# Two expert phases of a fused attention and expert network: choosing spread over units, low parts on GpSimd, a count copied by ScalarE, a weight load moved ahead, variances moved

## The chip, the cores and the metric

One core of one Trainium2 chip runs the whole program. The time is the device time of one execution in microseconds. Three executions of the kernel before took 2613.11, 2613.51 and 2613.93 us.

## The reference, cut to what matters

Two layers act on a residual x of 2048 rows (4 batches of 512) by 256.

```python
x = x + attention(layernorm(x), ctx)          # 16 heads of 64, 1024 context rows of 192, softmax
h = layernorm(x)                              # layer 0: 32 experts of width 128, 2 shared chunks
s = sigmoid(h @ gate.T); c = s + bias         # groups of 4: the best 4 of 8 groups, then the best 6 experts
w = chosen(s, c); w = 2.5 * w / sum(w)
x = x + sum_e w[:, e] * (silu(h @ g_e) * (h @ u_e)) @ d_e + shared(h)
x = x + attention(layernorm(x), ctx)
h = layernorm(x)                              # layer 1: 8 experts of width 512, 4 shared chunks
e = argmax(h @ router.T)                      # one expert a row
x = x + (silu(h @ g_e) * (h @ u_e)) @ d_e + shared(h)
```

## The kernel before, in words

The program runs five phases one behind the other, each a block with a barrier at its end: attention of layer 0 (tag L0a), experts of layer 0 (L0e), attention of layer 1 (L1a), shared experts and routing of layer 1 (L1e), and the routed experts of layer 1 on rows sorted by expert (L1s). Every fp32 operand of a product is split into a high part (a ScalarE copy to fp32r, a "_hi" tile) and a low part (a subtraction, "_lo"), and each product is three matmuls.

**Expert phase** (expert_phase). The weights come in chunks of 128 hidden columns, two buffers (raw[0] and raw[1]); four blocks of 512 rows each make a unit, so unit u is chunk u // 4 and block u % 4. Units are written out up to unit 9 and then looped eight at a time, or written out to unit 15 in layer 1. For a unit TensorE does gate_up (12 matmuls, L1365) into PSUM bank u % 2 and 2 + u % 2, ScalarE the silu of the gate (act_g, L1113), VectorE the product hid (L1176, counted by the semaphore mul), ScalarE the high part hid_hi (L1116, hhi), VectorE the low part hid_lo (L1181, hlo), and TensorE down (12 matmuls, L1379) of the unit two before; VectorE adds the result, weighted, to the residual (add, L1168, fma). gate_up(u) waits for mul of unit u - 2; down(u) waits for hlo of unit u and for the add of unit u - 2. VectorE's order in a unit is mul, add(u - 2), hid_lo. The weights of a chunk are split by ScalarE (split, L1102) at units 2, 6, 10, ... ahead of the silu, and by GpSimd (w_lo, L1083 and L1087); SyncE's queue loads the next chunk when w_lo has been made. In layer 1 the same queue carries two loads of 6 MB (prefetch) for the sorted phase.

**Choosing.** choose() is a Python generator of VectorE instructions that pick the experts, each linked to the one before it by a semaphore wait (link). In layer 0 it ends with the weights of the experts, which the adds need from unit 8 on. In layer 1 it goes on into sort_tokens: TensorE counts the rows of each expert (count, three matmuls into bank 1, L1393 and L1395), VectorE copies the counts out (L1231, L1232, semaphore taken), TensorE waits for that copy before gate_up(5), and more VectorE work makes slot_of, by which GpSimd scatters the rows to HBM at the end of its list (L1093). STEPS says how many pieces of the generator run ahead of which unit: those pieces stand before the unit's mul.

**Start of the phase.** ScalarE loads the square root's table (L1132), then makes rt_hi, the high part of the router (L1135); VectorE does four bn_stats (L1308), then rt_lo (L1310), for which TensorE's first matmuls (route, L1404) wait. raw[1] is loaded behind the bias, the sorted_x wipe of layer 0, and in layer 1 behind the first 6 MB.

**Attention phase** (attention_phase). A segment is a batch and a pair of heads, 32 in a phase, some 26 us each. VectorE's order in segment i is: low keys, statistics, variance at step 2 of a batch (ROOT, L578 to L583), inner_scales at step 3 (L590 to L592), outer_scales at step 4 (L596 to L598), then normalise, high and low output of segment i - 1 (L535 to L548), queries (L504, L509), low_rows, add_output (L558) and four row maxima (L530). GpSimd adds up the probabilities of the softmax in 14 additions of 128x512 (L326) in the middle of a segment.

Of the kernel before, what the change touches and what calls it, by code (L numbers as in the profile page):

```python
# [46 lines left out]
def build(nc, x, ctx_top, ctx_bot, layer_in, out):  # L47
# [6 lines left out]
    with stack:  # L54
# [37 lines left out]
        def attention_phase(tag, weights, value_weights, bias, xres, prefetch, source=None, again=False, keep=False, clear=()):  # L92

            with scope() as s:
# [29 lines left out]
                with nc.Block() as block:  # L124
# [373 lines left out]
                    def _(dve):  # L498
# [128 lines left out]
                        def segment(i):  # L627
# [9 lines left out]
                            if step == ROOT:  # L637
                                variance(b)
                            if step == INNER:
                                inner_scales(b)  # L640
                            if step == OUTER:
                                outer_scales(b)
# [9 lines left out]
                            if i + 1 < SEGMENTS:  # L652
                                high_queries(i + 1)
                                low_queries(i + 1)
                            if i > 0:
# [296 lines left out]
        def expert_phase(tag, cfg, bias, packed, xres, dispatch=None, prefetch=(None, None), wipe=None, clear=()):  # L952
# [9 lines left out]
            with scope() as s:  # L962
# [46 lines left out]
                with nc.Block() as block:  # L1009
# [20 lines left out]

                    def rest(eng, unit):

                        done = cfg["shared"] * BLK
                        first = -(-(done - 2) // ROUND)
                        for u in range(done, min(first * ROUND + 2, UNITS)):
                            unit((u - 2) // ROUND, (u - 2) % ROUND + 2)
# [4 lines left out]
                        if done < UNITS:  # L1041
# [4 lines left out]
                    def _(sp):  # L1046
                        if G:
# [9 lines left out]
                        sp.dma_start(raw[1], packed[1, :, :]).then_inc(sem["raw1"], 16)  # L1057
# [11 lines left out]
                    def _(pool):  # L1069
# [14 lines left out]
                        with pool.Fori(1, chunks // 2) as j:  # L1084
                            for par in range(2):
                                pool.wait_ge(sem["whi"], j * 2 + (par + 1))
                                nc.gpsimd.tensor_tensor(w_lo[:, par, :], raw[par], w_hi[:, par, :], ALU.subtract)\  # L1087
                                    .then_inc(sem["wlo"], 1)
# [10 lines left out]
                    def _(act):  # L1099
# [4 lines left out]
                        def unit(j, u):  # L1104
                            k = j * ROUND
                            if u % BLK == 2 and not (isinstance(j, int) and j == ROUNDS - 1 and u == ROUND - 2):
# [25 lines left out]
                        nc.scalar.activation(junk[:, :], ones[:, 0:1], ACT.Sqrt)  # L1132
                        act.wait_ge(sem["rt"], 16)
                        act.wait_ge(sem["pad"], 2)
                        nc.scalar.activation(rt_hi[:, :, 0:E], rt, ACT.Copy).then_inc(sem["rhi"], 1)  # L1135
                        split(0, 0)
# [10 lines left out]
                        unit(0, 0)  # L1147
                        unit(0, 1)
# [8 lines left out]
                    def _(dve):  # L1157
# [40 lines left out]
                        def pick(v, k, n, eq, gt, sel, start):  # L1198
# [6 lines left out]
                            if G:  # L1205
                                yield
# [557 lines left out]
```

## Time and profile before

| | us |
|---|---|
| median of three runs | 2613.51 |
| the profiled execution | 2618.82 |
| its span, first to last instruction | 2616.9 |
| TensorE busy | 2520.7 (96%) |
| VectorE busy | 2091.2 (80%) |
| GpSimd busy | 1482.1 (57%) |
| ScalarE busy | 1246.1 (48%) |

Times of the trace are microseconds from the span's start. The mean granted clock of TensorE is 0.985 of full speed over the span. A busy share of 96% says that TensorE almost never stands still; what it does wait for is found in the view of waits and in its timeline, where a bracket behind an instruction gives the idle time ahead of it and what ended that.

### The profile page before, as it was taken

Reading aid. Unit: us, or ns where it says so; the run is one execution under the profiler, and the core shown is the slowest. Engines: PE = TensorE matmul, PEld = TensorE weight load, DVE = VectorE, ACT = ScalarE, POOL = GpSimd, SP = SyncE. Lnnn points to the kernel's source line nnn. Section 1 sums busy time; section 2 is a strip of 40 time slices with the busy share of each in tenths; the row PEclk is TensorE's granted clock in tenths of the full one; section 3 lists DMA queues with packets and bytes.
Section 4 is the critical chain, followed back from the end, with each engine's and each line's share of the span. In section 5 each row is a group of like instructions: output and inputs, shape, how many; then the busy total and the mean of one; then the engine's idle time right before and its main releaser. Section 6 shows DMA issues by size and latency. Waiting matters only on the chain. (4 is left out here: it accounts for less than half of the span.)

```text
span 2616.9 us, 37958 instructions
## 1 busy us (share of the span) xinstructions
PE 2520.7 (96%) x13304; PEld 1776.5 (68%) x13304; DVE 2091.2 (80%) x2602; ACT 1246.1 (48%) x1774; POOL 1482.1 (57%) x1124
## 2 busy tenths in 40 slices
PE   8999999999999889999999899999999999998795
PEld 6666565656665678888888766666666665656684
DVE  7888888888888487777777788888888888866695
ACT  5555555555554323333333355455555454533393
POOL 5878777877777311111111187687878777760345
PEclk9999999999999999999999999999999999999897
DMA  4122212222221200000000121222131222115112
GB/s 147 45 59 53 63 45 58 63 49 50 63 51 41 72 19 24 24 24 24 24 24 18 47 75 45 55 61 59 45 79 45 59 53 55 45 29 235 47 54 88
DMA packets 118648, 145.09 MB, mean 55 GB/s; under 512 B 63856, under 2 KB 80112, under 8 KB 117488
## 3 DMA queue, kind: packets, MB, share of 16 engines
q1 hardware_dynamic: 113664, 136.10, 19.3%
q0 software_dynamic: 1536, 4.20, 0.5%
q10 hardware_dynamic: 3312, 3.02, 0.3%
q8 instruction: 81, 1.33, 0.2%
q14 instruction: 55, 0.45, 0.1%
HBM read 80.93 MB, written 11.80 MB: 35 GB/s over the span
## 5 line engine op out<-in xcount | busy, mean ns | idle before, releaser
L326 POOL TENSOR_TENSOR L1a_psums<-L1a_psums,L1a_probs 128x512 f32<-128x512 f32 x384 | 479.1, 1293 | 0.0
L326 POOL TENSOR_TENSOR L0a_psums<-L0a_psums,L0a_probs 128x512 f32<-128x512 f32 x384 | 478.8, 1289 | 0.0
L530 DVE TENSOR_REDUCE L1a_row_max<-psum 128x2 f32<-128x2048 f32 x128 | 293.6, 2293 | 59.2 <-PE psum L796 58.9
L530 DVE TENSOR_REDUCE L0a_row_max<-psum 128x2 f32<-128x2048 f32 x128 | 293.5, 2293 | 57.7 <-PE psum L796 57.2
L400 ACT ACTIVATE L0a_probs<-psum 128x1024 f32<-128x1024 f32 x256 | 251.6, 1027 | 105.9 <-PE psum L819 105.7
L400 ACT ACTIVATE L1a_probs<-psum 128x1024 f32<-128x1024 f32 x256 | 251.6, 1027 | 105.1 <-PE psum L819 104.9
L1168 DVE SCALAR_TENSOR_TENSOR xres<-psum,L0e_weights_of,xres 128x256 f32<-128x256 f32 x544 | 225.6, 478 | 22.6 <-PE psum L1379 21.7
L833 PE MATMUL psum<-L1a_probs,L1a_v 128*64 128x512 f32 x1024 | 240.5, 601 | 0.0
L833 PE MATMUL psum<-L0a_probs,L0a_v 128*64 128x512 f32 x1024 | 240.4, 601 | 0.0
L1365 PE MATMUL psum<-xnT_hi,L0e_w_hi 128*128 128x512 f32 x544 | 215.0, 395 | 9.4 <-DVE L0e_hid L1176 9.4
L1365 PE MATMUL psum<-xnT_lo,L0e_w_hi 128*128 128x512 f32 x544 | 214.6, 394 | 0.0
L1365 PE MATMUL psum<-xnT_hi,L0e_w_lo 128*128 128x512 f32 x544 | 213.1, 392 | 0.0
L818 PE MATMUL psum<-L0a_q_hh,L0a_k_st 128*128 128x512 f32 x512 | 204.4, 399 | 1.4 <-ACT L0a_probs L400 0.9
L818 PE MATMUL psum<-L1a_q_hh,L1a_k_st 128*128 128x512 f32 x512 | 204.3, 399 | 1.4 <-ACT L1a_probs L400 0.9
L819 PE MATMUL psum<-L1a_q_lm,L1a_k_hs 65*128 65x512 f32 x512 | 203.1, 397 | 0.0
L819 PE MATMUL psum<-L0a_q_lm,L0a_k_hs 65*128 65x512 f32 x512 | 203.0, 397 | 0.0
L1113 ACT ACTIVATE L0e_act_g<-psum 128x512 f32<-128x512 f32 x136 | 81.3, 598 | 243.4 <-PE psum L1365 243.4
L558 DVE TENSOR_TENSOR xres<-psum,xres 128x512 f32<-128x512 f32 x128 | 88.6, 692 | 114.9 <-PE psum L708 113.8
L1176 DVE TENSOR_TENSOR L0e_hid<-psum,L0e_act_g 128x512 f32<-128x512 f32 x136 | 93.7, 689 | 102.8 <-ACT L0e_act_g L1113 102.7
L326 POOL TENSOR_TENSOR L1a_psums<-L1a_probs 128x512 f32<-128x512 f32 x64 | 82.4, 1307 | 153.5 <-ACT L1a_probs L400 153.5
L1087 POOL TENSOR_TENSOR L0e_w_lo<-L0e_raw,L0e_w_hi 128x768 fp32r<-128x768 f32 x16 | 30.0, 1875 | 242.1 <-ACT L0e_w_hi L1102 242.1
L1087 POOL TENSOR_TENSOR L0e_w_lo<-ctx_stage,L0e_w_hi 128x768 fp32r<-128x768 f32 x16 | 30.6, 1914 | 240.9 <-ACT L0e_w_hi L1102 240.9
(384 smaller groups left out, 6148.6 us busy)
## 6 DMA issues: line engine op xcount, KB each, us to landing
L0a_k_hs<-L0a_k_st SPq DMA_DIRECT2D x64, 256.0 KB, 3.6
L1a_k_hs<-L1a_k_st SPq DMA_DIRECT2D x64, 256.0 KB, 3.7
L0a_raw<-in_attention SPq DMA_DIRECT2D x33, 384.0 KB, 3.4
L1a_raw<-in_attention SPq DMA_DIRECT2D x33, 384.0 KB, 3.4
L1weights<-in_sorted SPq DMA_DIRECT2D x2, 6144.0 KB, 20.6
L0a_q_hh<-L0a_q_hh SPq DMA_DIRECT2D x64, 128.0 KB, 2.3
L1a_q_hh<-L1a_q_hh SPq DMA_DIRECT2D x64, 128.0 KB, 2.3
ctx_stage<-in_experts SPq DMA_DIRECT2D x19, 384.0 KB, 3.0
```

The lines of the kernel that those rows point to most:

```text
L326: nc.gpsimd.tensor_tensor(psums[:, h, :], a, probs[:, h, kv, :], ALU.add).then_inc(sem["acc"], 1)
L400: nc.scalar.activation(probs[:, h, 2 * kp:2 * kp + 2, :], slot(h).rearrange("p (n q) -> p n q", n=2), ACT.Exp, scale=SCALE)\
L530: nc.vector.reduce_max(row_max[:, qt, 0:33:32], psum[:, 0:4 * BANK].rearrange("p (h k) -> p h k", h=2), axis=AX.X).then_inc(sem["max"], 1)
L558: nc.vector.tensor_tensor(rows, bank(PLACE[f"OUT{half}"]), rows, ALU.add).then_inc(sem["added"], 1)
L818: nc.tensor.matmul(dst, k_st[:, par, h, keys_of], q_hh[:, par, h, :], start=True, stop=False)
L819: last = nc.tensor.matmul(dst, k_hs[0:DH + 1, par, h, keys_of], q_lm[0:DH + 1, par, h, :], start=False, stop=True)
L833: last = nc.tensor.matmul(O[HEAD[h], :], v[:, pair % 2, kv, cols], probs[:, h, kv, :], start=kv == 0, stop=kv == KVT - 1)
L1087: nc.gpsimd.tensor_tensor(w_lo[:, par, :], raw[par], w_hi[:, par, :], ALU.subtract)\
L1113: nc.scalar.activation(act_g[:, u % 2, :], bank(u % 2), ACT.Silu).then_inc(sem["silu"], 1)
L1168: last = nc.vector.scalar_tensor_tensor(acc, bank(4 + 2 * (u % 2) + n // 2)[:, (n % 2) * DIM:(n % 2 + 1) * DIM], weights_of[:, ds(j * (2 * ...
L1176: nc.vector.tensor_tensor(hid[:, u % 2, :], bank(2 + u % 2), act_g[:, u % 2, :], ALU.mult)\
L1365: last = nc.tensor.matmul(bank(2 * g + u % 2), a[:, par, w], m[:, kd, rows], start=n == 0, stop=n == 3 * KD - 1)
```

## The change

1. The choosing of a phase is cut into eight pieces (layer 0) or seven (layer 1), one in each unit from unit 2 on, and a piece runs behind the unit's mul and ahead of its add, where it ran ahead of the mul before.
2. In units 2 to 9 (HELPED) GpSimd makes hid_lo; VectorE's mul of unit u then waits for hlo of unit u - 2. The w_lo of chunk 2 comes in GpSimd's list ahead of unit 6's hid_lo, that of chunk 3 behind unit 9's.
3. In layer 1 count goes into bank 0, behind gate_up(5), once the mul of unit 4 has been done; ScalarE makes both copies behind its unit 4; TensorE waits for them before gate_up(6), with down(3) in between.
4. raw[1] is the first DMA of the expert phase in SyncE's queue, and its split stands behind ScalarE's unit 0 instead of at unit 2.
5. rt_hi comes ahead of the square root's table load, and rt_lo ahead of the bn_stats.
6. In attention variance, inner_scales and outer_scales run behind the queries' low parts instead of ahead of normalise.

```diff
--- before.py
+++ after.py
@@ -634,12 +634,6 @@
                 statistics(b, step)
-            if step == ROOT:
-                variance(b)
-            if step == INNER:
-                inner_scales(b)
-            if step == OUTER:
-                outer_scales(b)
             if i == 0:
@@ -652,6 +646,12 @@
                 low_queries(i + 1)
+            if step == ROOT:
+                variance(b)
+            if step == INNER:
+                inner_scales(b)
+            if step == OUTER:
+                outer_scales(b)
             if i > 0:
@@ -1028,22 +1028,29 @@
+    SHARED_UNITS = cfg["shared"] * BLK
+    SINGLE = min(-(-(SHARED_UNITS - 2) // ROUND) * ROUND + 2, UNITS)
+    HELPED = range(2, 10)
+    COUNTED = 5
     def rest(eng, unit):
-        done = cfg["shared"] * BLK
-        first = -(-(done - 2) // ROUND)
-        for u in range(done, min(first * ROUND + 2, UNITS)):
-            unit((u - 2) // ROUND, (u - 2) % ROUND + 2)
+        first = -(-(SHARED_UNITS - 2) // ROUND)
         if first < ROUNDS - 1:
                     unit(j, u)
-        if done < UNITS:
+        if SHARED_UNITS < UNITS:
             for u in range(2, ROUND):
     def _(sp):
+        sp.dma_start(raw[1], packed[1, :, :]).then_inc(sem["raw1"], 16)
         if G:
@@ -1054,7 +1061,6 @@
                          zeros[:, :].unsqueeze(1).broadcast_to([P, wipe.shape[0] // P, DIM])).then_inc(sem["wiped"], 16)
-        sp.dma_start(raw[1], packed[1, :, :]).then_inc(sem["raw1"], 16)
         with sp.Fori(1, chunks // 2) as j:
@@ -1081,11 +1087,23 @@
         nc.gpsimd.tensor_tensor(w_lo[:, 1, :], raw[1], w_hi[:, 1, :], ALU.subtract).then_inc(sem["wlo"], 1)
-        with pool.Fori(1, chunks // 2) as j:
-            for par in range(2):
-                pool.wait_ge(sem["whi"], j * 2 + (par + 1))
-                nc.gpsimd.tensor_tensor(w_lo[:, par, :], raw[par], w_hi[:, par, :], ALU.subtract)\
-                    .then_inc(sem["wlo"], 1)
+        def low_weights(j, par):
+            pool.wait_ge(sem["whi"], j * 2 + (par + 1))
+            nc.gpsimd.tensor_tensor(w_lo[:, par, :], raw[par], w_hi[:, par, :], ALU.subtract)\
+                .then_inc(sem["wlo"], 1)
+        for u in HELPED:
+            if u % BLK == 2 and u > BLK and u < SHARED_UNITS:
+                low_weights(*divmod(u // BLK + 1, 2))
+            pool.wait_ge(sem["hhi"], u + 1)
+            nc.gpsimd.tensor_tensor(hid_lo[:, u % 4, :], hid[:, u % 2, :], hid_hi[:, u % 4, :], ALU.subtract)\
+                .then_inc(sem["hlo"], 1)
+        low_weights(1, 1)
+        if chunks > 4:
+            with pool.Fori(2, chunks // 2) as j:
+                for par in range(2):
+                    low_weights(j, par)
         if dispatch is not None:
@@ -1103,7 +1121,7 @@
             k = j * ROUND
-            if u % BLK == 2 and not (isinstance(j, int) and j == ROUNDS - 1 and u == ROUND - 2):
+            if u % BLK == 2 and not (isinstance(j, int) and (j, u) in ((0, 2), (ROUNDS - 1, ROUND - 2))):
                 c = u // BLK + 1
@@ -1129,10 +1147,10 @@
-        nc.scalar.activation(junk[:, :], ones[:, 0:1], ACT.Sqrt)
         act.wait_ge(sem["rt"], 16)
         nc.scalar.activation(rt_hi[:, :, 0:E], rt, ACT.Copy).then_inc(sem["rhi"], 1)
+        nc.scalar.activation(junk[:, :], ones[:, 0:1], ACT.Sqrt)
         split(0, 0)
@@ -1145,12 +1163,21 @@
         unit(0, 0)
+        split(0, 1)
         unit(0, 1)
                              ACT.Sigmoid if G else ACT.Copy).then_inc(sem["scores"], 1)
-        first_round(act, unit)
+        if dispatch is not None:
+            for u in range(2, COUNTED):
+                unit(0, u)
+            act.wait_ge(sem["counted"], 1)
+            nc.scalar.activation(held[:, :, :], bank(0)[:, NT * E:2 * NT * E].rearrange("p (t e) -> p e t", e=E), ACT.Copy)\
+                .then_inc(sem["taken"], 1)
+            nc.scalar.activation(gt[:, :, :], bank(0, NT * E).rearrange("p (t e) -> p t e", e=E), ACT.Copy)\
+                .then_inc(sem["taken"], 1)
+        first_round(act, unit, COUNTED if dispatch is not None else 2)
         other_rounds(act, unit)
@@ -1172,11 +1199,20 @@
             k = j * ROUND
+            number = k + u if isinstance(j, int) else None
             dve.wait_ge(sem["silu"], k + (u + 1))
+            if number is not None and number - 2 in HELPED:
+                dve.wait_ge(sem["hlo"], number - 1)
             nc.vector.tensor_tensor(hid[:, u % 2, :], bank(2 + u % 2), act_g[:, u % 2, :], ALU.mult)\
                 .then_inc(sem["mul"], 1)
+            if number in STEPS:
+                next(choosing, None)
             if u >= 2:
                 add(j, u - 2)
+            if number in HELPED:
+                return
+            if number == HELPED.stop:
+                dve.wait_ge(sem["hlo"], HELPED.stop)
             dve.wait_ge(sem["hhi"], k + (u + 1))
@@ -1202,15 +1238,13 @@
             link(last)
-            if G:
-                yield
+            yield
             kth = top[:, :, k - 1:k].broadcast_to([P, NT, n])
             link(nc.vector.tensor_scalar(need[:, :], need[:, :], -1.0, float(k), ALU.mult, ALU.add))
-            if G:
-                yield
+            yield
@@ -1221,19 +1255,14 @@
             nc.vector.memset(start[:, :, 0:1], 0.0).then_inc(sem["picked"], 1)
+            yield
             link(nc.vector.memset(index[:, :], 1.0))
             yield
-            dve.wait_ge(sem["counted"], 1)
-            link(nc.vector.tensor_copy(held[:, :, :], bank(1)[:, NT * E:2 * NT * E].rearrange("p (t e) -> p e t", e=E)))
-            nc.vector.tensor_copy(gt[:, :, :], bank(1, NT * E).rearrange("p (t e) -> p t e", e=E))\
-                .then_inc(sem["taken"], 1)
-            dve.wait_ge(sem["taken"], 1)
-            yield
+            dve.wait_ge(sem["taken"], 2)
             link(nc.vector.tensor_tensor_scan(upto[:, :, :].rearrange("p e t -> p (e t)"),
@@ -1304,10 +1333,10 @@
+        dve.wait_ge(sem["rhi"], 1)
+        nc.vector.tensor_tensor(rt_lo[:, :, 0:E], rt, rt_hi[:, :, 0:E], ALU.subtract).then_inc(sem["rlo"], 1)
         for n in range(NT - TAIL):
             nc.vector.bn_stats(stats[:, n, :], xres[:, TAIL + n, :]).then_inc(sem["stat"], 1)
-        dve.wait_ge(sem["rhi"], 1)
-        nc.vector.tensor_tensor(rt_lo[:, :, 0:E], rt, rt_hi[:, :, 0:E], ALU.subtract).then_inc(sem["rlo"], 1)
         dve.wait_ge(sem["stat"], NT - TAIL)
@@ -1336,13 +1365,12 @@
         choosing = choose()
-        STEPS = {3: 1, 4: 1, 5: 2, 6: 2, 7: 2} if G else {3: 1, 5: 1, 6: 2, 7: 1}
-        for u in range(cfg["shared"] * BLK):
-            for _ in range(STEPS.get(u, 0)):
-                next(choosing, None)
+        STEPS = range(2, 10) if G else range(2, 9)
+        for u in range(SINGLE):
             unit(u // ROUND, u % ROUND) if u < 2 else unit((u - 2) // ROUND, (u - 2) % ROUND + 2)
             pass
+        dve.wait_ge(sem["hlo"], HELPED.stop)
         rest(dve, unit)
@@ -1387,14 +1415,13 @@
             pe.wait_ge(sem["const"], 2)
-            pe.wait_ge(sem["mul"], 2 + 4)
+            pe.wait_ge(sem["mul"], 2 + COUNTED)
             pe.wait_ge(sem["picked"], 1)
             picked = sel[:, :, :].rearrange("p t e -> p (t e)")
-            nc.tensor.matmul(bank(1)[:, 0:NT * E], earlier, picked, start=True, stop=True)
+            nc.tensor.matmul(bank(0)[:, 0:NT * E], earlier, picked, start=True, stop=True)
             for part in (slice(0, DH), slice(DH, P)):
-                last = nc.tensor.matmul(bank(1)[part, NT * E:2 * NT * E], ones[:, :], picked, start=True, stop=True)
+                last = nc.tensor.matmul(bank(0)[part, NT * E:2 * NT * E], ones[:, :], picked, start=True, stop=True)
             last.then_inc(sem["counted"], 1)
-            pe.wait_ge(sem["taken"], 1)
@@ -1444,8 +1471,11 @@
         if dispatch is not None:
+            gate_up(0, COUNTED)
             count()
-        first_round(pe, unit, 5)
+            down(0, COUNTED - 2)
+            pe.wait_ge(sem["taken"], 2)
+        first_round(pe, unit, COUNTED + (dispatch is not None))
         other_rounds(pe, unit)
```

## Rows read from the trace of the kernel before

**Rows 1.** The page's busy times of the whole span.

```profile
PE 2520.7 (96%) x13304; PEld 1776.5 (68%) x13304; DVE 2091.2 (80%) x2602; ACT 1246.1 (48%) x1774; POOL 1482.1 (57%) x1124
```

**Rows 2.** TensorE's waits, whole span: total us, times, longest us.

```profile
PE psum L1365 <- DVE L0e_hid L1176: 9.4, 5, 4.1
PE psum L1379 <- DVE L1e_hid_lo L1181: 4.7, 1, 4.7
...
PE psum L708 <- DVE L0a_o_split L548: 3.2, 5, 1.1
...
PE psum L708 <- DVE L1a_o_split L548: 1.6, 3, 0.6
```

**Rows 3.** Timeline of TensorE, L0e: gate_up of units 4, 8, 10 and 12.

```profile
911.20 0.47 PE L1365 MATMUL psum<-xnT_hi,L0e_w_hi 128*128 128x512 f32 x1 [1.08 <-DVE L0e_hid L1176]
...
938.46 0.47 PE L1365 MATMUL psum<-xnT_hi,L0e_w_hi 128*128 128x512 f32 x1 [4.15 <-DVE L0e_hid L1176]
...
948.95 0.40 PE L1365 MATMUL psum<-xnT_hi,L0e_w_hi 128*128 128x512 f32 x1
...
957.31 0.40 PE L1365 MATMUL psum<-xnT_hi,L0e_w_hi 128*128 128x512 f32 x1
```

**Rows 4.** VectorE in L0e: muls of units 2, 6, 7, 8; a scan.

```profile
910.37 0.69 DVE L1176 TENSOR_TENSOR L0e_hid<-psum,L0e_act_g 128x512 f32<-128x512 f32 x1 [7.53 <-ACT L0e_act_g L1113]
...
934.18 1.23 DVE L1215 TENSOR_TENSOR_SCAN L0e_sel<-L0e_start,L0e_eq 128x512 f32<-128x512 f32 x1
...
937.62 0.69 DVE L1176 TENSOR_TENSOR L0e_hid<-psum,L0e_act_g 128x512 f32<-128x512 f32 x1
...
943.92 0.69 DVE L1176 TENSOR_TENSOR L0e_hid<-psum,L0e_act_g 128x512 f32<-128x512 f32 x1
...
946.69 0.69 DVE L1176 TENSOR_TENSOR L0e_hid<-psum,L0e_act_g 128x512 f32<-128x512 f32 x1
```

**Rows 5.** The first instructions of L0e on ScalarE and GpSimd: rt_hi, the pads.

```profile
885.90 0.24 ACT L1135 ACTIVATE L0e_hid_lo<-ctx_stage 128x64 fp32r<-128x64 f32 x1
...
884.57 0.57 POOL L1072 MEMSET L0e_hid_lo<- 128x256 f32 x2 [10.11 <-POOLq L124]
```

**Rows 6.** Timeline of ScalarE, L0e: split of chunk 1 and the silu's table.

```profile
907.59 0.84 ACT L1102 ACTIVATE L0e_w_hi<-L0e_raw 128x768 fp32r<-128x768 f32 x1
908.44 1.28 ACT L1113 ACT_TABLE_LOAD   x1
```

**Rows 7.** VectorE and GpSimd at the same time in L0e.

```profile
931.02 2.20 DVE L1209 TENSOR_TENSOR L0e_eq<-L0e_choice,L0e_late 128x512 f32<-128x512 f32 x1
...
929.69 2.98 POOL L1087 TENSOR_TENSOR L0e_w_lo<-ctx_stage,L0e_w_hi 128x768 fp32r<-128x768 f32 x1 [19.34 <-ACT L0e_w_hi L1102]
```

**Rows 8.** Timeline of L1e: split; gate_up 4, count, gate_up 5 and 6.

```profile
2382.61 0.84 ACT L1102 ACTIVATE L1e_w_hi<-L1e_raw 128x768 fp32r<-128x768 f32 x1 [2.45 <-DMA L1e_raw<-in_experts]
...
2385.41 0.50 PE L1365 MATMUL psum<-xnT_hi,L1e_w_hi 128*128 128x512 f32 x1 [2.49 <-POOL L1e_w_lo L1083]
...
2392.82 0.46 PE L1393 MATMUL psum<-L1e_sel,ctx_stage 128*128 128x128 f32 x2 [1.36 <-issue]
...
2398.23 0.80 PE L1365 MATMUL psum<-xnT_hi,L1e_w_hi 128*128 128x512 f32 x1 [4.58 <-DVE L1e_gt L1232]
...
2404.79 0.39 PE L1365 MATMUL psum<-xnT_hi,L1e_w_hi 128*128 128x512 f32 x1
```

**Rows 9.** Timeline, L0a: VectorE in a ROOT and the next segment, then GpSimd.

```profile
298.69 1.49 DVE L578 TENSOR_TENSOR L0a_total_of<-L0a_stats 128x8 f32<-128x8 f32 x1
...
300.98 3.36 DVE L535 RECIPROCAL L0a_inv<-psum 128x512 f32<-128x512 f32 x1
...
310.67 1.40 DVE L558 TENSOR_TENSOR xres<-psum,xres 128x512 f32<-128x512 f32 x2 [1.42 <-PE psum L708]
...
336.89 1.40 DVE L558 TENSOR_TENSOR xres<-psum,xres 128x512 f32<-128x512 f32 x2 [2.25 <-PE psum L708]
...
303.82 14.97 POOL L326 TENSOR_TENSOR L0a_psums<-L0a_psums,L0a_probs 128x512 f32<-128x512 f32 x12
```

## The prediction

> **What bounds the kernel now.** The page's busy times come first: TensorE works 96% of the span [rows 1]. An edit that only unloads another engine is worth nothing but where TensorE waits for it. So the view of TensorE's waits comes next [rows 2]: 9.4 us for VectorE's products in L0e, 4.7 us at the end of L1e, and waits of 0.53 us each for o_split, four in L0a ((3.2 - 1.1) / 4; the 1.1 is the phase's last segment) and three in L1a. The timeline of TensorE shows what those waits cost with what follows them. In L0e, gate_up(10) starts at 948.95 and gate_up(12) at 957.31, so an undisturbed unit takes 4.18 us; the six from gate_up(4) at 911.20 should take 25.1 us and took 37.75 [rows 3]: 12.7 us are lost. In L1e, gate_up(4) starts at 2385.41 and gate_up(6) at 2404.79, 19.4 us for two units of 8.4 [rows 8]; part of that is the clock, since the first matmul behind the 4.58 us wait took 0.80 us and one of the same shape later 0.39, the two lengths of TensorE's lower and upper level (1.2 and 2.4 GHz).
>
> Why VectorE is late in L0e: a unit without choosing takes it 2.77 us (946.69 - 943.92): 0.61 mul, 1.57 add, 0.60 hid_lo by their pitches. From the mul of unit 2 at 910.37 to that of unit 7 at 943.92 there are 33.55 us; less five times 2.77 that leaves 19.7 us of choosing, 1.5 of it a stall (below), so 18.2 us of work [rows 4]. Because a piece stands ahead of the mul, the next gate_up waits for all of it; the largest lump, ahead of 937.62, gives the wait of 4.15 us [rows 3, 4].
>
> **L0e, the start.** rt_hi needs the pads, done at 885.14 (884.57 + 0.57), but starts at 885.90 behind a table load [rows 5]. It moves up by some 0.7 us, rt_lo and TensorE's first matmul with it. The table load, split, bn_stats and variance behind it come up to 0.9 us later; they have cover, since TensorE has 18 route matmuls and 12 of gate_up(0) ahead of the transposes that need them. I take 0.7 us in both expert phases, bounds 0 and 0.8.
>
> **The split of chunk 1.** Now 0.84 us of split and 1.28 us of table load lie between scores and silu(2) [rows 6]; the split goes behind unit 0, where the w_lo(1) and TensorE's later gate_ups cover it. Gain 0.8 us up to gate_up(4). With the start it lands at 911.20 - 0.7 - 0.8 = 909.7. The wipe and the bias in SyncE's queue come behind a load of 384 KB, which nobody near waits for.
>
> **L0e, the units.** VectorE's unit is now 0.61 + 1.57 = 2.18 us plus a piece. The same 18.2 us cut at the yields give 3.1, 1.2, 2.3, 2.3, 2.4, 3.4, 1.4, 2.1 us for units 2 to 9; the sixth is the scan at 934.18 and three operations up to 937.62, 3.44 us [rows 4]. The mul of unit 2 starts at 908.9. What TensorE waits for is no longer mul but the add ahead of down: down(7) needs add(5), in unit 7. To there VectorE needs six units of 2.18 and six pieces, 13.1 + 14.7 = 27.8 us, and 0.5 us for semaphores and full-length muls: 937.2. A unit-by-unit walk with TensorE beside it gives the same, with a first wait of 2 us at down(2) for add(0).
>
> **The price of GpSimd's half.** Sum and range hang on this. GpSimd's subtraction of 128x512 costs 1.25 us by the pitch of the L326 run (14.97 / 12) [rows 9], against 0.60 on VectorE; it is there some 2.1 us behind mul (0.7 for hid_hi, by ScalarE's 0.84 us for one and a half times the columns [rows 6], then 1.3 and a semaphore), and gate_up(u + 2) covers that: it streams twice the columns of down, so of a unit's 4.18 us I estimate 2.75 for it and 1.43 for down. But the engines block each other: a w_lo recorded as 2.98 us ran beside a VectorE comparison of 2.20 us, 1.5 more than the 0.69 of its like [rows 7], so GpSimd waited through VectorE's running pair of operations, and then VectorE's next waited. The stall comes only if VectorE's next operation reads two SBUF tensors: the run of L326 stands beside VectorE operations with a PSUM operand that keep their length, such as L535 and L558 [rows 9]. GpSimd comes 0.7 us behind the end of mul. In pieces 1, 2, 4 and 7 VectorE then does reductions or maxima, or has finished; in 3 and 6 (the chains of scan and comparisons) it is blocked once, for 1.15 us; 5 and 8 are at the edge. I take two blocks, 2.3 us. Then down(7) runs from 939.6, gate_up(10) from 941.0, against 948.95: **7.9 us** for the whole phase with its start. Bounds: no block, 10.2 us; a block in all eight, 1.4 us.
>
> The Trainium skill speaks against this step. Perfetto Trace Analysis, Optimizing Scalar/DVE Operations, says that moving work between GpSimd and VectorE "might not help" because they share a read port; SBUF — State Buffer, Who interferes with whom, makes it an exclusive lock for an instruction's length when VectorE reads two SBUF inputs. By that rule taken for every unit, the gain in L0e is the 1.4 us of the bound; the trace agrees on the lock, with the 2.20 us.
>
> **L1e.** raw[1] now lands only behind a 6 MB load: the split at 2382.61 waited for the DMA and gate_up(4) waited 2.49 us for GpSimd's w_lo [rows 8]. Issued first, it is there 15 us early; all of the 2.49 goes, and gate_up(4) starts at 2385.41 - 2.49 - 0.7 = 2382.2. Then TensorE: gate_up(4) and down(2), 4.18; gate_up(5), 2.75, to 2389.2; count wants the mul of unit 4 and piece 3 (1.5 us). VectorE gets there at 2389.5, or 1.15 later if GpSimd blocks it once, as in L0e; I take the block. So count starts at 2390.7, takes some 0.85 (its first two of six records took 0.46 [rows 8]), down(3) 1.43, under which ScalarE makes its two copies of 128x128, some 0.3 us each; ScalarE's unit 5 waits for them and has 2 us in hand. gate_up(6) starts at 2393.0 instead of 2404.79: **11.8 us**, bounds 10.7 and 12.9. No wait is left that is as long as the 4.58 us, so I expect the upper clock level. Behind it TensorE is at its pitch; the scatter stays tied to unit 10 and moves along. The second 6 MB go out 9 us earlier with w_lo(1); only L1s needs them.
>
> **Attention.** A variance starts at 298.69 and delays normalise to 300.98, 2.29 us, 1.3 of it a block by GpSimd's w_lo [rows 9]; that is the 0.53 us wait of TensorE. Moved, it stands in VectorE's idle time ahead of L558, but under GpSimd's run of twelve additions. Idle there: 1.42 + 2.29 - 0.54 = 3.17 us. The chain is 1.24 us of work with three reads of two SBUF tensors behind a link: 0.5 us of block for the first by the phase of the run, 1.1 for each further one, 3.9 in all. It overruns by 0.8 at most, and VectorE has 0.2 to 0.4 us in hand before the next scores; I take 0.2 us of stall, so 0.33 is gained seven times: **2.3 us**. The pieces of INNER and OUTER need 2.4 us and find 2.25 + 0.6 [rows 9]: nothing. Bounds: 3.7 us gained with no overrun; 6 us lost with a full block at each of the eight.
>
> **The sum.** 7.9 + 11.8 + 2.3 = 22.0 us. The span goes from 2616.9 to 2594.9, the profiled execution from 2618.8 to 2596.8, and the median, 5.3 below that, from 2613.5 to **2591.5**.
>
> **Rivals.** (a) The full lock: every piece is blocked, L0e gives 1.4, L1e 10.7 and attention about 0: 12 us, 2601. For it, the 2.20 us; against it, reductions and PSUM operands under the run of L326. Chance 0.17.
> (b) The wait at L1e's end [rows 2]: 4.7 us come from VectorE and ScalarE standing still beside GpSimd's scatter with nothing of the program to wait for. Moved code may be rid of it, 2587, or meet it once more, 2596. Chance 0.15.
> (c) Slower: VectorE's small chains behind the queries don't get in between two of GpSimd's twelve additions but wait for two more. The run's pitch (1.25) is shorter than what one addition records (1.29), as in VectorE's pair, through which GpSimd waited. Place: 24 segments of both attentions. Price: 2.5 us each less 0.5 in hand for INNER and OUTER, 8 x 2.5 + 16 x 2.0 = 52, so 2643. It decides once the mean delay passes 22 / 24 = 0.9 us a segment. Against it: L578's 1.49 us ended 0.1 us before the end of the w_lo that blocked it, which leaves a gap. Chance 0.04.
> (d) The change does nothing: the waits only turn up behind DMA or clock, within 0.2% (5 us). The full units show no such bound. 0.02.
>
> **The numbers.** Forecast 0.62, the rest as above. 0.2% is about what a measurement of this kernel can tell from no change. The range takes in (a) and (b) and the bounds of L0e: 2583 to 2602; likeliest 2591.5. Faster 0.94, same 0.02, slower 0.04.
>
> **What would show it.** Right: gate_up(10) of L0e some 8 us earlier relative to the phase's start; waits of TensorE for L1168 (add) at down(2) and down(7) in place of those for L1176; VectorE's operations in pieces 3 and 6 lengthened by 1.15; no wait for w_lo or count over 1.5 us in L1e; waits for o_split gone in the ROOT segments. Wrong: L326 or the maxima lengthening the segments, or down waiting for GpSimd's hid_lo.

## The result, and the profile after

The changed kernel takes **2633.99 us** (median of 4 runs, 2630.36 to 2635.35) against 2613.31 (2611.55 to 2613.93) of the kernel before: ratio 1.0078, 95% interval 1.0061 to 1.0096. It is slower by 20.7 us, where 22 us of gain were forecast. The profiled execution took 2632.88 us, its span is 2630.7.

The page's busy times of the kernel after answer to [rows 1]. TensorE is busy longer with the same number of instructions (2528.1 for 2520.7 us) and its mean granted clock is 0.982 where it was 0.985, so more of them ran at the lower clock level; VectorE has 18 instructions fewer and 60 us more, so something stretches them:

```profile
PE 2528.1 (96%) x13304; PEld 1780.7 (68%) x13304; DVE 2151.3 (82%) x2584; ACT 1246.2 (47%) x1776; POOL 1501.2 (57%) x1140
```

TensorE's waits after, as in [rows 2] (total us, times, longest):

```profile
PE psum L796 <- DVE L0a_row_max L530: 14.1, 4, 3.5
PE psum L796 <- DVE L1a_row_max L530: 14.1, 4, 3.5
PE psum L1407 <- DVE xres L1195: 5.3, 5, 2.1
...
PE psum L1421 <- DVE L1e_start L1257: 2.2, 1, 2.2
```

The 9.4 us in front of gate_up are gone but for 0.35, as forecast, and 5.3 us in front of down (for add, now L1195) stand in their place. New are the first two lines: eight waits of 3.5 us in attention, one in each ROOT segment of both layers. Segments are 26.24 us long, 26.67 where rows are prepared; the ROOT segments took 27.0 to 27.1 before (one 26.24) and take 31.3 to 32.7 after. From a matmul of the first segment to the same one of the last (L802), the two attentions grew from 820.5 and 819.8 us to 840.3 and 840.9: **40.9 us lost there**.

The timeline of VectorE in the ROOT segment of [rows 9], after. L578 to L583 is the variance, now behind the queries (L504, L509):

```profile
309.58 1.39 DVE L509 TENSOR_TENSOR L0a_q_lm<-psum,L0a_q_hh 64x512 fp32r<-64x512 f32 x2
311.00 0.65 DVE L578 TENSOR_TENSOR L0a_total_of<-L0a_stats 128x8 f32<-128x8 f32 x1
311.58 1.31 DVE L579 TENSOR_TENSOR L0a_var<-L0a_stats 128x8 f32<-128x8 f32 x1
312.82 1.33 DVE L580 TENSOR_TENSOR L0a_dif<-L0a_stats 128x8 f32<-128x8 f32 x1
314.19 1.20 DVE L581 SCALAR_TENSOR_TENSOR L0a_dif<-L0a_dif 128x8 f32<-128x8 f32 x1
315.43 1.20 DVE L582 TENSOR_TENSOR L0a_var<-L0a_var,L0a_dif 128x8 f32<-128x8 f32 x1
316.66 1.20 DVE L583 TENSOR_SCALAR L0a_var<-L0a_var 128x8 f32<-128x8 f32 x1
317.89 1.29 DVE L558 TENSOR_TENSOR xres<-psum,xres 128x512 f32<-128x512 f32 x2
```

GpSimd's twelve additions run under them at a pitch of 1.24 us (14.89 / 12), and TensorE then waits for the row maximum behind L558:

```profile
307.83 14.89 POOL L326 TENSOR_TENSOR L0a_psums<-L0a_psums,L0a_probs 128x512 f32<-128x512 f32 x12
...
321.43 1.22 PE L796 MATMUL psum<-L0a_k_st,L0a_q_hh 64*128 64x512 f32 x4 [3.52 <-DVE L0a_row_max L530]
322.58 0.79 PE L708 MATMUL psum<-ctx_hi,L0a_w_split 128*128 128x512 f32 x1
...
327.15 0.85 PE L796 MATMUL psum<-L0a_k_st,L0a_q_hh 64*128 64x512 f32 x4
```

Six instructions on 8 columns: the first lasts as long as the rest of one of GpSimd's additions, the other five about as long as a whole one, 6.9 us for a chain that takes 0.9 where nothing holds it (the run with the variance at step 3, below). In all eight ROOT segments each of the six ends 0.02 to 0.03 us behind the end of an addition of GpSimd. And the wait isn't the whole price: TensorE stood still for 3.52 us, and the granted clock of the stretch behind it, from 321.43 to 327.15, is 0.50, the lower of the two levels (1.2 GHz). From 322.58 to 327.15 the ten matmuls took 4.57 us; where there was no wait the same ten take 2.5 (below).

In the expert phases the forecast came about. L0e, TensorE: the first route matmul, gate_up(4), down(2), down(7), gate_up(10):

```profile
906.22 0.50 PE L1431 MATMUL psum<-xnT_hi,L0e_hid_lo 128*128 128x512 f32 x1 [1.57 <-DVE L0e_hid_lo L1337]
...
928.61 0.47 PE L1393 MATMUL psum<-xnT_hi,L0e_w_hi 128*128 128x512 f32 x1 [0.35 <-DVE L0e_hid L1206]
...
933.26 0.36 PE L1407 MATMUL psum<-L0e_w_hi,L0e_hid_hi 128*128 128x256 f32 x1 [1.69 <-DVE xres L1195]
...
958.85 0.52 PE L1407 MATMUL psum<-L0e_w_hi,L0e_hid_hi 128*128 128x256 f32 x1 [2.10 <-DVE xres L1195]
...
961.52 0.63 PE L1393 MATMUL psum<-xnT_hi,L0e_w_hi 128*128 128x512 f32 x1
```

The phase begins 19.8 us later than before, so places are compared from its first route matmul (886.45 before). gate_up(10) stood 62.50 us behind it [rows 3] and stands 55.30 behind it: 7.20 won, with 0.64 for the start itself (TensorE waited 2.21 us for rt_lo before, 1.57 after) 7.84. In L1e, gate_up(6) stood 44.24 us behind the first matmul (2404.79 [rows 8] less 2360.55) and stands 33.87 behind it (2426.07 less 2392.20): 10.37, and 11.0 with its start. The wait for w_lo is gone, and count waits 2.17 us. TensorE in L1e, gate_up(4), count and gate_up(6):

```profile
2414.42 0.39 PE L1393 MATMUL psum<-xnT_hi,L1e_w_hi 128*128 128x512 f32 x1
...
2423.77 0.46 PE L1421 MATMUL psum<-L1e_sel,ctx_stage 128*128 128x128 f32 x2 [2.17 <-DVE L1e_start L1257]
...
2426.07 0.39 PE L1393 MATMUL psum<-xnT_hi,L1e_w_hi 128*128 128x512 f32 x1
```

These are places in one execution each. In another profile of the old expert phases (part 6 alone, below) the two distances are 63.22 and 44.98. Other profiles of the new ones (the first, third and fifth run below) put gate_up(10) 54.14, 55.14 and 55.31 us behind the first route matmul, and gate_up(6) of L1e 35.33, 35.29 and 33.85: in the two with 35.3 the granted clock falls to 0.5 behind the wait for count, in the profile after it doesn't.

### The profile page after: what moved, and what is told of

Same layout as the page of the kernel before. It is cut to its first block and busy times, and to the rows that moved or that the text cites. A ratio compares the mean times of both kernels' runs of the same rounds, so it can differ in the third digit from the quotient of the medians.

```text
span 2630.7 us, 37948 instructions
## 1 busy us (share of the span) xinstructions
PE 2528.1 (96%) x13304; PEld 1780.7 (68%) x13304; DVE 2151.3 (82%) x2584; ACT 1246.2 (47%) x1776; POOL 1501.2 (57%) x1140
## 3 DMA queue, kind: packets, MB, share of 16 engines
q8 instruction: 81, 1.33, 0.2%
## 5 line engine op out<-in xcount | busy, mean ns | idle before, releaser
L1195 DVE SCALAR_TENSOR_TENSOR xres<-psum,L0e_weights_of,xres 128x256 f32<-128x256 f32 x544 | 225.6, 477 | 22.3 <-PE psum L1407 21.1
L326 POOL TENSOR_TENSOR L1a_psums<-L1a_probs 128x512 f32<-128x512 f32 x64 | 82.4, 1307 | 153.9 <-ACT L1a_probs L400 153.9
L326 POOL TENSOR_TENSOR L0a_psums<-L0a_probs 128x512 f32<-128x512 f32 x64 | 82.4, 1308 | 147.2 <-ACT L0a_probs L400 147.2
L1407 PE MATMUL psum<-L0e_w_hi,L0e_hid_hi 128*128 128x256 f32 x544 | 154.5, 284 | 6.2 <-DVE xres L1195 5.3
```

The source lines that it names most:

```text
L326: nc.gpsimd.tensor_tensor(psums[:, h, :], a, probs[:, h, kv, :], ALU.add).then_inc(sem["acc"], 1)
L1195: last = nc.vector.scalar_tensor_tensor(acc, bank(4 + 2 * (u % 2) + n // 2)[:, (n % 2) * DIM:(n % 2 + 1) * DIM], weights_of[:, ds(j * (2 * ...
L1407: last = nc.tensor.matmul(dst, a[:, u % 4, rows], b[:, par, w], start=m == 0, stop=m == 2)
```

## The experiments

Theory: the variance behind the queries costs about 41 us, all else gains about 20. First rival: the lengthening belongs to attention as a whole (scales and variance together). Second: part of the loss is in the expert phases, in GpSimd's half.

**Without part 6, and part 6 alone.** The six lines go back ahead of add_bias in the changed kernel, and in the second run they alone are moved in the kernel before:

```diff
@@ segment(i), from the changed kernel
+if step == ROOT:
+    variance(b)
+if step == INNER:
+    inner_scales(b)
+if step == OUTER:
+    outer_scales(b)
 if i == 0:
     add_bias(0)
...
 low_queries(i + 1)
-if step == ROOT:
-    variance(b)
-if step == INNER:
-    inner_scales(b)
-if step == OUTER:
-    outer_scales(b)
```

> The change without its sixth part: variance, inner_scales and outer_scales stand ahead of normalise again. Theory A (in the ROOT segments each of VectorE's six small instructions waits out one of GpSimd's additions; the segments went from 27.0 to 31.3 to 32.7 us and the two attentions grew by 19.8 and 21.1 us): the whole 40.9 us goes, 2634.0 - 40.9 = 2593. Theory B (the loss comes from GpSimd's halves or from moved code in the expert phases): the time stays above 2613. My forecast for the other parts by themselves was 19.7 us of gain, 2593.6.

> The kernel before with the sixth part alone. Theory A: 2613.3 + 40.9 = 2654, with the same eight waits of 3.5 us for the row maxima. Theory B: near 2613, or a little under it.

Measured: without part 6 **2592.88 us** (2591.3 to 2593.76), ratio 0.9926 (0.9912 to 0.9939); part 6 alone 2651.06 (2647.84 to 2652.75), ratio 1.0146 (1.013 to 1.0161). The two changes to the time, -19.2 and +39.0 against the kernel before measured beside them (2612.03), add up to 19.8; the whole change made 20.7. The timeline of VectorE without part 6 shows the chain in its old place, between the keys (L521) and normalise (L535): one block of 1.3 us, from GpSimd's w_lo, then five free instructions.

```profile
298.53 1.39 DVE L521 TENSOR_TENSOR L0a_k_st<-psum,L0a_k_st 64x512 fp32r<-64x512 f32 x2
299.95 1.47 DVE L578 TENSOR_TENSOR L0a_total_of<-L0a_stats 128x8 f32<-128x8 f32 x1
301.35 0.16 DVE L579 TENSOR_TENSOR L0a_var<-L0a_stats 128x8 f32<-128x8 f32 x1
...
302.03 0.17 DVE L583 TENSOR_SCALAR L0a_var<-L0a_var 128x8 f32<-128x8 f32 x1
302.23 3.36 DVE L535 RECIPROCAL L0a_inv<-psum 128x512 f32<-128x512 f32 x1
```

TensorE in the same place of that kernel, with no wait; from 316.55 to 319.07 its ten matmuls take 2.52 us instead of 4.57:

```profile
315.89 0.73 PE L796 MATMUL psum<-L0a_k_st,L0a_q_hh 64*128 64x512 f32 x4
316.55 0.50 PE L708 MATMUL psum<-ctx_hi,L0a_w_split 128*128 128x512 f32 x1
...
319.07 0.73 PE L796 MATMUL psum<-L0a_k_st,L0a_q_hh 64*128 64x512 f32 x4
```

So this ROOT segment pays 3.5 us of waiting and 2.5 of clock (2.05, and 0.49 of the first L796). All eight wait 3.5 us. What is left of their length over 26.24 is put down to the clock: 1.5 to 1.6 us in the three segments of 31.3 to 31.4, 2.5 to 2.9 in the five of 32.2 to 32.7, 2.3 in the mean. That makes 5.8 each, 46.3 in all, less the 0.8 that the old place costs in seven: 41. **The second rival falls**: L0e took 592.30 us here and 593.34 in the changed kernel.

**The scales alone behind the queries.** The kernel without part 6, with inner_scales and outer_scales moved and the variance left:

```diff
-if step == INNER:
-    inner_scales(b)
-if step == OUTER:
-    outer_scales(b)
 if i == 0:
...
 low_queries(i + 1)
+if step == INNER:
+    inner_scales(b)
+if step == OUTER:
+    outer_scales(b)
```

> As the first of these runs, but inner_scales and outer_scales stay behind the queries; only variance is back. Theory A: three instructions a segment with at most two blocks fit in the idle time ahead of add_output, so no difference to the first run (within 1 us). Rival: they cost some 0.5 us in each of 16 segments, 8 us more.

Measured: 2592.8 us (2591.87 to 2595.98), ratio 0.9929 (0.9915 to 0.9942), the same as without part 6. Its timeline of VectorE in an INNER segment shows why: two blocked instructions, and still 1.02 us of idle time in front of L558. In the OUTER segment all three are blocked (0.66, 1.20 and 1.22 us) and only 0.21 us is left, the last line. The first rival falls too; it is the variance alone.

```profile
334.31 0.41 DVE L591 TENSOR_TENSOR L0a_dif<-L0a_var,L0a_rstd 128x8 f32<-128x8 f32 x1
334.76 1.20 DVE L592 TENSOR_TENSOR L0a_dif<-L0a_dif,L0a_rstd 128x8 f32<-128x8 f32 x1
336.97 1.35 DVE L558 TENSOR_TENSOR xres<-psum,xres 128x512 f32<-128x512 f32 x2 [1.02 <-PE psum L708]
...
363.67 1.29 DVE L558 TENSOR_TENSOR xres<-psum,xres 128x512 f32<-128x512 f32 x2 [0.21 <-DVE L0a_shift L598]
```

**No half on GpSimd.** The kernel without part 6, with VectorE making every hid_lo:

```diff
-for u in HELPED:
-    ...
-    nc.gpsimd.tensor_tensor(hid_lo[:, u % 4, :], hid[:, u % 2, :], hid_hi[:, u % 4, :], ALU.subtract)\
-        .then_inc(sem["hlo"], 1)
+low_weights(1, 0)
 low_weights(1, 1)
@@ VectorE's unit
-if number is not None and number - 2 in HELPED:
-    dve.wait_ge(sem["hlo"], number - 1)
...
-if number in HELPED:
-    return
```

> As the first run, but VectorE makes every hid_lo again and GpSimd none; the choosing stays spread behind the mul. Theory A: GpSimd's half saves VectorE 0.6 us a unit and costs it a block of 0.3 to 1.1 us in five of eight units, so it is worth nothing: the time is that of the first run within 1 us. Rival: the half is what brings the gain in L0e, and the time rises by 3 to 5 us.

Measured: 2591.13 us (2589.69 to 2594.79), ratio 0.9922 (0.9909 to 0.9936), against 2592.88 with the half. L0e takes 592.9 us (592.3 with it). **The half is worth nothing.** In the changed kernel GpSimd's operation took 0.6 us of work from each of VectorE's units; the timeline of VectorE in L0e shows what it gave back, one stretched operation in each of units 3, 4, 7 and 9 (their free lengths are 0.17, 0.29, 0.69 and 0.63 us), and one at 950.06 in unit 6 by 0.26 us:

```profile
934.59 1.19 DVE L1246 TENSOR_SCALAR L0e_need<-L0e_need 128x16 f32<-128x16 f32 x1
...
939.09 1.26 DVE L1253 TENSOR_TENSOR L0e_gsel<-L0e_ggt,L0e_geq 128x128 f32<-128x128 f32 x1
...
953.95 1.60 DVE L1251 TENSOR_TENSOR L0e_sel<-L0e_sel,L0e_need 128x512 f32<-128x512 f32 x1
...
964.25 1.60 DVE L1325 COPY L0e_weights_of<-L0e_sel 128x512 f32<-128x512 f32 x1
```

That is 1.02 + 0.97 + 0.26 + 0.91 + 0.97 = 4.1 us of the 8 x 0.6 = 4.8 taken off, and the first four, 3.2 us, come ahead of gate_up(10). In L1e the half costs TensorE time. count waits 2.16 to 2.18 us in the six profiles with the half, 1.43 and 1.40 in the two without it; the timeline of TensorE in this run:

```profile
2382.23 0.46 PE L1409 MATMUL psum<-L1e_sel,ctx_stage 128*128 128x128 f32 x2 [1.43 <-DVE L1e_start L1246]
```

The Trainium skill, in Perfetto Trace Analysis, Optimizing Scalar/DVE Operations, says that moving work between these two engines "might not help". The run agrees, 2591.13 us without the move against 2592.88. What gained in L0e is then the order (pieces behind mul), with the start and the split; none of these was undone by itself here, so how they share the gain is not shown.

**The variance where GpSimd pauses.** The scales' place makes room: the kernel without part 6, everything ahead of normalise, with the steps

```diff
-NEXT_STATS, LAST_STATS, ROOT, INNER, OUTER, BIAS = 0, 1, 2, 3, 4, 7
+NEXT_STATS, LAST_STATS, ROOT, INNER, OUTER, BIAS = 0, 1, 3, 4, 4, 7
```

> As the run with the variances back, but ROOT, INNER and OUTER are 3, 4 and 4 instead of 2, 3 and 4: variance stands ahead of normalise in the segment in which VectorE's instructions of inner_scales met no addition of GpSimd, and the two scales go together one segment later. Theory A: unblocked, 1.24 us ahead of normalise fit in the slack (2.29 us cost 0.5), so seven segments of 27.0 us become 26.2: 5.5 us less than that run, 2587. Rival: any work ahead of normalise costs TensorE a wait, and the two scales (1.2 us) add one; no gain or a small loss.

Measured: 2588.71 us (2585.14 to 2591.04), ratio 0.9912 (0.9897 to 0.9928). That is 24.7 us under the kernel before beside it (2613.4), where the kernel without part 6 was 19.2 under its own: 5.5 more, as forecast. The two intervals overlap, but the seven segments that shrink by 0.8 us each carry the same sum. In that segment GpSimd ends its w_lo at 320.35 (318.53 + 1.82) and then stands idle for 6.40 us, until the additions begin at 326.75; the variance falls into that gap, and the timelines of VectorE and GpSimd show all six instructions free:

```profile
324.12 0.17 DVE L578 TENSOR_TENSOR L0a_total_of<-L0a_stats 128x8 f32<-128x8 f32 x1
...
324.90 0.17 DVE L583 TENSOR_SCALAR L0a_var<-L0a_var 128x8 f32<-128x8 f32 x1
...
326.75 1.29 POOL L326 TENSOR_TENSOR L0a_psums<-L0a_probs 128x512 f32<-128x512 f32 x1 [6.40 <-ACT L0a_probs L400]
```

Every ROOT segment is 26.24 us long. So the same six instructions cost 0 in this place, 0.8 us in the old one and 5.8 in the new one (a mean of 32.0 less 26.24): the place against GpSimd's work makes the price, not the instructions. Free, the chain takes 0.95 us here (324.12 to 325.07).

**Part 4 alone.** raw[1] first in SyncE's queue, its split behind unit 0, in the kernel before:

```diff
+sp.dma_start(raw[1], packed[1, :, :]).then_inc(sem["raw1"], 16)
 if G:
...
-sp.dma_start(raw[1], packed[1, :, :]).then_inc(sem["raw1"], 16)
@@ ScalarE
 unit(0, 0)
+split(0, 1)
 unit(0, 1)
```

> The kernel before with the fourth part alone (raw[1] first in SyncE's queue, its split behind unit 0). My sum: 2.5 us in L1e (the wait for w_lo goes) and 0.8 us in L0e, 3.3 us: 2608.7 beside 2612.0. Rival: the wait for the chosen experts further on absorbs both, within 1 us of before.

Measured: 2608.48 us (2603.33 to 2610.49, 11 runs; before 2613.4), ratio 0.9982 (0.9973 to 0.9991). In L0e TensorE's wait for gate_up(4) falls from 1.08 to 0.36 us. In L1e the 2.49 us for w_lo are gone and the 4.58 us behind count stay. In front of count stand 2.62 us; the same expert phases as before had 1.36 there in the profile before and 2.92 in that of part 6 alone, so it isn't shown that any of the 2.49 came back. Against these two profiles gate_up(10) of L0e stands 0.7 and 1.4 us nearer to its first route matmul, gate_up(6) of L1e 1.2 and 2.0, 1.9 to 3.4 together. The forecast was 3.3, the measured 4.9 has an interval from 2.4 to 7.1; the rival's 1 us falls. TensorE in L1e:

```profile
2390.98 0.46 PE L1394 MATMUL psum<-L1e_sel,ctx_stage 128*128 128x128 f32 x2 [2.62 <-DVE L1e_hid L1177]
2396.39 0.79 PE L1366 MATMUL psum<-xnT_hi,L1e_w_hi 128*128 128x512 f32 x1 [4.58 <-DVE L1e_gt L1233]
```

**Both together.** The variance at step 3, no half on GpSimd:

> The run without GpSimd's half (2591.1) with ROOT, INNER and OUTER at 3, 4 and 4. If the two add up: 2591.1 - 5.5 = 2585.6.

Measured: **2586.13 us** (2585.86 to 2586.9, 4 runs), ratio 0.99 (0.9885 to 0.9916). That is the forecast of 2585.6 within 0.5. It beats both kernels, by 27 and 48 us.

**Which instructions wait.** The kernel without part 6, with seven independent instructions on 4 columns behind the queries of each batch's step 4; their results are not used:

```diff
+if step == 4:
+    two = (bias_sb[:, 0:4], bias_sb[:, 4:8])
+    nc.vector.tensor_tensor(probe[:, 0, :], two[0], two[1], ALU.add)
+    nc.vector.tensor_tensor(probe[:, 1, :], two[0], two[1], ALU.add)
+    nc.vector.tensor_scalar(probe[:, 2, :], two[0], 2.0, 1.0, ALU.mult, ALU.add)
+    nc.vector.reciprocal(probe[:, 3, :], two[0])
+    nc.vector.memset(probe[:, 6, :], 0.0)
+    nc.vector.tensor_copy(probe[:, 7, :], two[0])
+    nc.vector.reduce_sum(probe[:, 8, 0:1], two[0], axis=AX.X)
```

> As the run with the variances back, with seven independent instructions of 128x4 elements behind the queries at step 4 of each batch, under GpSimd's run of additions; their results are not used. Theory A, by what the changed kernel's records show: both tensor_tensor (SBUF, SBUF), tensor_scalar and tensor_copy (one SBUF input each) record 1.0 to 1.3 us, although nothing links them; reciprocal, reduce_sum and memset record 0.1 to 0.2 us. Rival: only instructions behind a semaphore wait are caught, the others pass as one group behind the first.

Measured: 2663.2 us, one run. Two of the eight places look like this one:

```profile
149.22 1.17 DVE L658 TENSOR_TENSOR L0a_probe<-L0a_bias_sb 128x4 f32<-128x4 f32 x1
150.31 1.33 DVE L659 TENSOR_TENSOR L0a_probe<-L0a_bias_sb 128x4 f32<-128x4 f32 x1
151.57 1.33 DVE L660 TENSOR_SCALAR L0a_probe<-L0a_bias_sb 128x4 f32<-128x4 f32 x1
152.81 0.17 DVE L661 RECIPROCAL L0a_probe<-L0a_bias_sb 128x4 f32<-128x4 f32 x1
152.91 1.21 DVE L663 COPY L0a_probe<-L0a_bias_sb 128x4 f32<-128x4 f32 x1
...
154.04 0.14 DVE L664 TENSOR_REDUCE L0a_probe<-L0a_bias_sb 128x1 f32<-128x4 f32 x1
```

Both additions wait, though nothing links them, and so do tensor_scalar and the copy with their single SBUF input; reciprocal, memset and reduction don't. The other six places look like this, first VectorE, then GpSimd:

```profile
363.25 11.01 DVE L658 TENSOR_TENSOR L0a_probe<-L0a_bias_sb 128x4 f32<-128x4 f32 x1
374.18 0.15 DVE L659 TENSOR_TENSOR L0a_probe<-L0a_bias_sb 128x4 f32<-128x4 f32 x1
...
361.87 12.37 POOL L327 TENSOR_TENSOR L0a_psums<-L0a_psums,L0a_probs 128x512 f32<-128x512 f32 x10
```

The first addition ends with GpSimd's run (361.87 + 12.37 = 374.24), having waited through nine of GpSimd's fourteen additions, and TensorE waits 8.7 us. With the run over, nothing holds the others. The Trainium skill has the rule in SBUF — State Buffer, Who interferes with whom: the first to issue holds the shared port for its whole instruction, two SBUF inputs of VectorE contend, and so can copies and tensor_scalar, while reductions never do. The 1.33 and 0.14 us agree; that a wait may outlast one instruction of the other engine is shown by this run and the next.

**What decides between one addition and all.** One 128x4 addition in 32 places (steps 3 to 6 of each batch), behind reductions of 0 to 1200 columns that shift its arrival; results not used:

```diff
+if 3 <= step <= 6:
+    number_of = 4 * b + step - 3
+    width = 80 * number_of if tag[1] == "0" else 1200 - 80 * number_of
+    for k, w in enumerate([240] * (width // 240) + [width % 240] * (width % 240 > 0)):
+        nc.vector.reduce_sum(probe[:, 8 - k // 4, k % 4:k % 4 + 1], bias_sb[:, 0:w], axis=AX.X)
+    nc.vector.tensor_tensor(probe[:, 0, :], bias_sb[:, 0:4], bias_sb[:, 4:8], ALU.add)
```

> A single 128x4 addition of two SBUF inputs behind the queries of steps 3 to 6 of each batch (32 places), after 0 to 1200 columns of VectorE reductions (one SBUF input, which GpSimd's additions did not hold up in the probe before), so that it arrives at another point of GpSimd's 1.25 us pitch each time. Theory A (the point of arrival decides): arrivals within about 0.2 us of the start of one of GpSimd's additions may be held until the run of additions ends (up to 11 us), all others are held for the rest of that one addition, so 0.2 to 1.3 us, and the durations follow the arrival on a slope of -1. Theory B (what stands in VectorE's queue ahead decides, a reduction or the pair of operations of the queries): the length of the hold does not follow the arrival; then single additions behind reductions are held once wherever they arrive, and those without a reduction ahead (width 0) to the end of the run. Time: 2593 and up to 9 us for each long hold; with none, about 2595.

Measured: 2764.47 us, one run on another chip, where the kernel before took 2617.57. 17 places were held for the rest of one addition, 15 for 9.6 to 11.1 us. Two that arrived at the same point of GpSimd's addition, one of either kind, each with the row of GpSimd around it (the first holds two additions; arrivals 0.53 and 0.54 us behind the start):

```profile
357.85 2.55 POOL L327 TENSOR_TENSOR L0a_psums<-L0a_psums,L0a_probs 128x512 f32<-128x512 f32 x2
358.38 10.61 DVE L661 TENSOR_TENSOR L0a_probe<-L0a_bias_sb 128x4 f32<-128x4 f32 x1
...
655.64 1.30 POOL L327 TENSOR_TENSOR L0a_psums<-L0a_psums,L0a_probs 128x512 f32<-128x512 f32 x1
656.18 0.79 DVE L661 TENSOR_TENSOR L0a_probe<-L0a_bias_sb 128x4 f32<-128x4 f32 x1
```

**Both theories fall.** The short holds do shrink by what the arrival is late (0.79 us at 0.54, down to 0.16), but the same point of arrival gave both kinds, and both stand behind reductions. What sorts them best is the segment: all 8 places in step 3 were long, 5 of 8 in step 4, 2 of 8 in step 5, none of 8 in step 6. But the segment doesn't decide alone: in the probe before, all eight first additions stood in step 4, came 0.12 to 0.15 us into the sixth of GpSimd's fourteen additions, and six were long, two short. What decides stays open.

## Why the prediction was wrong

**The step that failed** is the attention term, "the chain is 1.24 us of work with three reads of two SBUF tensors behind a link: 0.5 us of block for the first by the phase of the run, 1.1 for each further one, 3.9 in all. It overruns by 0.8 at most". The block per instruction was sized well (1.03 to 1.16 beyond the first, 0.5 for the first). The count was wrong, three instead of six. L579 and L580 have no link, and I let them follow L578 through one gap; each waited for the end of another addition. And L583, with one SBUF input, was taken as free. The 1.24 us of work comes from no row that is shown; free, the chain takes 0.91 to 0.95. Held, it took 6.9 us and overran the 3.17 by 3.7, TensorE waited 3.5, and the lower clock behind that wait, which had no term at all, added 2.3 in the mean. The maxima lengthening the segments, which the prediction names as a sign of being wrong, are the two new lines of waits. The bound of 6 us lost for the eight segments was 0.75 each; it allowed one more block, where six held instructions were the bound that the form of the code gave. Forecast 2.3 us gained, measured 40.9 lost.

**Rival (c)** named the right engine pair and the right sign with a chance of 0.04, but for 24 segments and two further additions at once. In the changed kernel the 16 segments of the scales cost nothing, as the forecast itself said, but partly by luck: for 2.4 us forecast their chains took 1.9 (INNER) and 3.1 (OUTER), and the second fitted with 0.21 to spare. The eight others cost 5 us each. Its condition, a mean delay over 0.9 us a segment, was met: 41 / 24 = 1.7. The argument against it, a gap between two of GpSimd's instructions, is true for a single wait, and says nothing of how often a chain must find one. Its mechanism in the strict sense (a wait through more than one addition) turned up in the probes.

**L0e**: forecast 7.9 us, measured 7.84 at gate_up(10); to the first matmul of L1a it is 6.8 (600.16 to 593.34), 7.5 with the start. Start: 0.7 forecast, 0.64 measured. Split: 0.8 forecast, 0.72 (1.08 less 0.36). First wait at down(2): 2 us forecast, 1.69 measured. Blocks ahead of gate_up(10): two of 1.15 forecast, four measured with 3.2 us in all. Those in pieces 3 and 6 came (0.97 and 0.91); that in piece 2 (L1246) hit a tensor_scalar of one SBUF input, the kind that was taken as free in the variance too. So the agreement is partly luck, the same phase gave 9.0 in another profile (54.14), and forecasting a gain from the half was wrong. The prediction's bound of 1.4 us takes eight blocks at 1.1; at its own 1.15 it is 1.0.

**L1e**: forecast 11.8 us at gate_up(6) with bounds of 10.7 and 12.9, measured 11.0 in the profile after and 9.6 in two others, where the clock fell. count waited 2.17 us where the times of the forecast give 1.5, which is 0.7 of the missing 0.8; without the half it waited 1.4, so the half cost 0.75 at this place, net of the work that it takes off VectorE. The forecast expected the upper clock level because no wait as long as 4.58 us was left. It held in the profile after, but not in those two, behind 2.18 us.

**Rival (b)**, the wait of 4.7 us at the end of L1e: it is 0.9 us in the profile after and in those of the first seven runs, that with part 6 alone among them, whose L1e is that of before. In the profile of the last run, whose L1e is that of the first, a wait of 2.6 us turns up again. So the code doesn't fix it; it belongs to single executions, and the profiled one of the kernel before was also 5.3 us above its median. What brings it about stays open.

**Rival (a)**, the full lock in every piece, would have left 12 us in the expert phases; without part 6 it was 19.2 (2612.03 - 2592.88), for 19.7 forecast, so it falls there. But its mechanism is what attention showed, where it was priced at about 0: every instruction of the variance was held. (d), no change, falls by the 19.2 and the 41 alike.

## What to carry to other kernels

Count every VectorE instruction of a small chain that will stand under a back-to-back stream on GpSimd, even one of 4 or 8 columns: each two-input, tensor_scalar or copy operation on SBUF cost one of GpSimd's instructions here, so a chain of six cost six, and in the probes one could cost nine. Move such chains to where GpSimd is idle (six free instructions at step 3), rather than to where VectorE is idle. And price a long TensorE wait with the matmuls behind it that run at the lower clock, here 1.5 to 2.9 us on top of 3.5.

## What the runs showed of the hardware that was not expected

- A VectorE instruction with 4 columns was held for 9.6 to 11.1 us, to the end of GpSimd's run of additions, in 21 of 40 probed places, and for the rest of one addition (0.16 to 1.35 us) in the other 19. The point of arrival within an addition doesn't decide it, nor does the segment alone: eight additions at the same point of the same addition in step 4 were long six times and short twice.
- Where the first of several VectorE instructions was held once, each later two-input, tensor_scalar or copy operation was held once too (1.17, 1.33, 1.33 and 1.21 us at 149.22), while reciprocal, memset and reduction kept 0.17, 0.06 and 0.14; where it was held to the end of the run, the others were free.
- Two instructions without a link between them were each held for one addition: 1.31 and 1.33 us for L579 and L580.
